# Mask rows in the score stacks, maxima sent round once a batch, and a five-step attention plan on one Trainium2 core

## The reference

```python
xn = _layernorm(x)
x = x + _L0_attn_ref(xn, ...) + _L0_ffn_ref(xn, ...)
xn = _layernorm(x)
x = x + _L1_attn_ref(xn, ...) + _L1_ffn_ref(xn, ...)
# attention, 16 heads of 8 channels, causal (layer 1: 4 key/value heads, rotary)
scores = jnp.einsum('bhqd,bhkd->bhqk', q, k) / jnp.sqrt(D)
scores = jnp.where(causal, scores, -jnp.inf)
out = jnp.einsum('bhqk,bhkd->bhqd', softmax(scores), v)
# experts: 8 of width 512, the top 2 of each token
# layer 0: at most 40 places per expert and batch, relu, softmax gates
# layer 1: no limit, gelu, the two gates by a softmax over their logits
```

## Time and profile before

| | |
|---|---|
| three runs, us | 520.85, 519.69, 522.8; median 520.85 |
| the profiled execution | 522.24 us, span 520.2 us, mean granted clock 0.96 |
| PE busy | 452.7 us, 87% of the span, 3503 matmuls |
| PE weight loads | 343.1 us, 66% |
| DVE | 322.6 us, 62%, 974 instructions |
| ACT | 248.0 us, 48% |
| POOL | 173.7 us, 33% |
| DMA | 45.89 MB, mean 88 GB/s |

### The profile page before, as it was taken

The page is one execution under the profiler, slowest core; times in us unless marked ns, Lnnn a source line. Parts: engine busy times, 40 slices in busy tenths (PEclk is TensorE's granted clock), DMA queues, the critical chain, the costliest instruction groups (busy, mean ns, idle before and its releaser), DMA issues.

```text
span 520.2 us, 10264 instructions
## 1 busy us (share of the span) xinstructions
PE 452.7 (87%) x3503; PEld 343.1 (66%) x3503; DVE 322.6 (62%) x974; ACT 248.0 (48%) x564; POOL 173.7 (33%) x226
## 2 busy tenths in 40 slices
PE   1668899979999999999988987894999999898985
PEld 1554567758868878677665663663999997554643
DVE  5565741126668868777787795642666665565672
ACT  1731455524655655454464442442565563644452
POOL 6640120003254354444544417771000000737600
PEclk9998999997999999999999997896999999899898
DMA  5553123473223233021162612231221211314220
GB/s 163 134 129 89 63 64 107 122 211 114 68 74 99 69 90 115 15 79 42 42 202 95 192 59 70 87 97 56 62 81 44 81 58 36 102 43 135 52 58 28
DMA packets 51441, 45.89 MB, mean 88 GB/s; under 512 B 4968, under 2 KB 46464, under 8 KB 51392
## 3 DMA queue, kind: packets, MB, share of 16 engines
q1 hardware_dynamic: 47424, 35.54, 23.9%
q0 software_dynamic: 2240, 4.53, 3.2%
q10 hardware_dynamic: 1728, 5.20, 3.0%
HBM read 26.24 MB, written 19.01 MB: 87 GB/s over the span
## 4 chain that ended last, share of the span: by engine, by line
PE 49%; issue 23%; DVE 9%; POOL 8%; DMA 5%; ACT 3%; SPq 1%; ACTq 0%; DVEq 0%; POOLq 0%
PE ps_S L1498 7%; PE ps_P L1520 6%; POOL xs L742 6%; PE ps_N L1469 6%; PE ps_N L1465 4%; PE ps_M L1717 3%; PE ps_M L1563 2%; PE ps_M L1600 2%; PE ps_P L1537 2%; DMA X<-in_L_attn_x 2%; PE ps_P L1554 2%; DVE NM L1059 2%; PE ps_N L1710 2%; PE ps_S L1710 2%; PE ps_M L1574 1%
## 5 line engine op out<-in xcount | busy, mean ns | idle before, releaser
L824 ACT ACTIVATE PT<-ps_S 128x512 f32<-128x512 f32 x192 | 112.6, 592 | 98.5 <-PE ps_S L1498 96.6
L1059 DVE TENSOR_REDUCE NM<-ps_N 128x2 f32<-128x512 f32 (+1 forms) x192 | 128.0, 682 | 46.0 <-PE ps_N L1469 44.8
L1469 PE MATMUL ps_N<-STK 96*128 96x256 f32 (+1 forms) x256 | 103.2, 446 | 0.0
L689 POOL TENSOR_SCALAR_AFFINE_SELECT PT<-PT 128x512 f32<-128x512 f32 x80 | 49.1, 638 | 142.5 <-ACT PT L824 142.5
L1498 PE MATMUL ps_S<-STK 100*128 100x128 f32 (+5 forms) x352 | 92.8, 339 | 3.2 <-ACT PT L824 3.2
L1465 PE MATMUL ps_N<-maskb,identb 128*128 128x256 bf16 (+1 forms) x192 | 62.2, 324 | 6.7 <-DVE NM L1059 6.3
L1498 PEld LDWEIGHTS ps_S<-STK 104*128 104x128 f32 (+1 forms) x352 | 62.3, 199 | 7.5 <-ACT PT L824 4.5
L1520 PE MATMUL ps_P<-PT,VA 128*32 128x256 f32 (+1 forms) x1024 | 56.8, 341 | 0.4 <-ACT PT L824 0.4
L1469 PEld LDWEIGHTS ps_N<-STK 96*128 96x128 f32 x256 | 52.0, 203 | 4.7 <-issue 0.7
L731 POOL TENSOR_TENSOR ROT<-ROT 128x256 f32<-128x256 f32 (+1 forms) x16 | 11.3, 731 | 104.2 <-DVE ROT L1088 104.2
L1520 PEld LDWEIGHTS ps_P<-PT,VA 128*32 128x32 f32 x1024 | 27.2, 111 | 26.8 <-issue 12.6
(11 more groups left out here) (197 smaller groups left out, 818.3 us busy)
## 6 DMA issues: line engine op xcount, KB each, us to landing
STK<-scr SPq DMA_DIRECT2D x96, 96.0 KB
scr<-XQ SPq DMA_DIRECT2D x24, 256.0 KB
ROT<-in_L_ffn_W SPq DMA_DIRECT2D x16, 256.0 KB, 3.1
EW<-in_moe ACTq DMA_DIRECT2D x8, 512.0 KB, 3.4
scr<-XQ SPq DMA_DIRECT2D x24, 128.0 KB
xs<-zero SPq DMA_DIRECT2D x1, 2496.0 KB, 11.1
LATE<-xs SPq DMA_DIRECT2D x9, 256.0 KB, 2.8
ysl<-LATE SPq DMA_DIRECT2D x9, 256.0 KB, 2.3
```

Of the source, the lines that this page charges most:

```text
L689: last = pool.affine_select(out=v, in_=v, compare_op=ALU.is_ge, fill=0.0, base=0, pattern=[[0, 4], [1, P]], channel_multiplier=-1)
L824: act.activation(PT[:, g, r, :], bank[s][:], ACT.Exp, scale=SCALE).then_inc(exp_ok, 1)
L1059: dve.tensor_reduce(NM[b % 2][:, h, qt, :].rearrange("q (p c) -> q c p", p=2)[:, slots[0]:slots[-1] + 1, :], bank[s][:].rearrange("q (c p ...
L1469: last = mm(s[:, 2 * w_ * i:2 * w_ * (i + 1)], stk[0:QK_ROWS, c, P * qt:P * (qt + 1)], stk[0:QK_ROWS, k_slots(L, c, 2 * h, 2), 0:w_], star ...
```

## The change

**Mask rows.** The stack's rows 96 to 127 now also carry constants (`constant_rows`, from 512 more columns of the table): rows 104 and up are built so that the product of a query's and a key's row is hugely negative where the key comes after the query. `nat` no longer lays a mask; the diagonal block of 128 keys is multiplied over all 128 rows of the stack, the block left of it over 96. Rows 96 to 103 of the query side have to be zero until the maxima come, so from the fourth batch on SP first copies zeros into them (`L578`).

**Maxima once.** `mxt`, the split, `scm` and the way into the stack handle 16 heads at once, when all twelve units are done: one DMA out and one in, where there were two and four. All of `st` now waits for them.

**The plan.** `st` of a batch runs from unit 4 of its step to unit 3 of the next; `otr`, `ott`, `proj`, `res` come a step later (`e`), `otr` in two halves; there are four buffers of values and two of OT. In steps after the first `qk` stands at unit 2 (was 0), `stack` at unit 5 or 6 (was 1), `mxt` at 0, `px` at unit 4 (was 9), `py` at 6 (4), `po` at 10 (5), `pl` at 7 (10). The slots move from unit 5 to unit 11 of step 12, the scatters to two units each, `moe` from behind step 13 to unit 8 of step 15, and the gathers to one unit each behind it. The plan has 20 steps, was 19.

```diff
+            for i in range(P):
+                for j in range(-(-P // MBLK)):
+                    row, at = ST_ROWS + j, i % MBLK
+                    if i // MBLK == j:
+                        t[row, [CO_KM + i, CO_KM + P + i]] = 2.0 ** (22 * at - 107)
...
-FFN_AFTER, MOE_AFTER = 2, 13
+YC_AT = (9, 11, 15, 17, 22, 25, 40, 44)
+FFN_AFTER, MOE_AFTER = 2, 15
...
         for u in range(12):
-            if u == 0:
+            if u == (0 if first else 2):
                 add("qk", a)
+            if a and u == (0 if first else 3 + 2 * a[0]):
                 add("hi", a)
-            if a and u == a[0]:
+            if a and u == (0 if first else 4 + 2 * a[0]):
                 add("lo", a)
...
             add("nat", b, u)
-            add("st", c, u // 3, u % 3)
+            s, v = (c, u - ST_AT) if u >= ST_AT else (d, u + 12 - ST_AT)
+            add("st", s, v // 3, v % 3)
             add("max", b, u)
...
             if u == 0:
-                add("pv", d, 3)
+                add("mxt", c)
+                add("pv", d, 1)
             if u == 1:
-                add("mxt", c, 1)
-                add("mrow", c, 1)
-                add("stack", a)
-                add("ocp", d, 1)
+                add("mrow", c)
+                add("ocp", d, 0)
+            if u == (1 if first else 5 + a[0] if a else None):
+                add("stack", a)
...
             if u == 4:
-                layer1("py", e)
                 ffn0("disp", g)
                 ffn0("gm", g)
+                layer1("px", k)
...
+            at = 12 * (t - NB - 5) + u
+            if 0 <= at < 2 * NT and at % 2 == 0:
+                plan.append(("scat", at // 2))
+            at = 12 * (t - MOE_AFTER) + u - 9
+            if 0 <= at < NT:
+                plan.append(("back", at))
...
                 if n >= NSTK:
                     await_full(sp, "S1", ("st", *back(L, b, NSTK), 3, 2))
+                    sp.dma_start(stk[QK_ROWS:ST_ROWS, 0:KS, :], stk[0:ST_ROWS - QK_ROWS, KS + 1:KS + 2, :]
+                                 .broadcast_to((ST_ROWS - QK_ROWS, KS, T))).then_inc(stk_in[s], 16)
...
-                diag = s[:].rearrange("q (h k) -> q h k", h=many)[:, :, w_ - P:w_]
-                mm(diag, identb[:], maskb[:, None, :].broadcast_to((P, many, P)), start=True, stop=False,
-                   skip_group_check=True)
                 stk = STK[seq(L, b) % NSTK]
+                q, k = slice(P * qt, P * (qt + 1)), slice(w_ - P, w_)
                 for i, c in enumerate(slots):
-                    last = mm(s[:, 2 * w_ * i:2 * w_ * (i + 1)], stk[0:QK_ROWS, c, P * qt:P * (qt + 1)],
-                              stk[0:QK_ROWS, k_slots(L, c, 2 * h, 2), 0:w_], start=False, stop=True, skip_group_check=True)
+                    o = s[:, 2 * w_ * i:2 * w_ * (i + 1)].rearrange("q (h k) -> q h k", h=2)
+                    if qt > 0:
+                        mm(o[:, :, 0:P], stk[0:QK_ROWS, c, q], stk[0:QK_ROWS, k_slots(L, c, 2 * h, 2), 0:P], start=True, stop=True)
+                    last = mm(o[:, :, k], stk[:, c, q], stk[:, k_slots(L, c, 2 * h, 2), k], start=True, stop=True)
                 last.then_inc(full[f"N{u % 2}"], 1)
```

More of the change, by code:

```diff
@@ L182, in attention_plan @@
                     plan += [("lg",), ("route",)]
[L183 to L191, removed]
-                plan += [("scat", i) for i in range((6, 9, 11, 14, 16)[u // 3], (6, 9, 11, 14, 16)[u // 3 + 1])]
@@ L193, in attention_plan @@
-            if NB + 6 <= t < NB + 9 and u % 3 == 2:
-                k = 4 * (t - NB - 6) + u // 3
-                plan += [("back", i) for i in range(NT * k // 12, NT * (k + 1) // 12)]
-            if t == NB + 8 and u in (6, 8):
-                plan.append(("yc", u // 2 - 3))
-            if t == NB + 9 and u in (0, 2, 4, 6, 7, 9):
-                plan.append(("yc", {0: 2, 2: 3, 4: 4, 6: 5, 7: 6, 9: 7}[u]))
             if u == 4:
-                layer1("py", e)
                 ffn0("disp", g)
@@ L223, in attention_plan @@
             if u == 10:
-                add("ocp", c, 0)
-                layer1("pl", e)
-            if u == 11:
-                add("pv", c, 2)
+                add("otr", d, 1)
+                add("norm", d, 1)
+                layer1("po", h)
+            if t == NB + 4 and u in (8, 9):
+                plan.append(("r1" + "cd"[u - 8],))
+            if t == NB + 4 and u == 10:
+                plan.append(("rank",))
+            if t == NB + 4 and u == 11:
+                plan.append(("slots",))
+            at = 12 * (t - NB - 5) + u
[4 more added lines that the diff above has]
+                plan.append(("back", at))
+            if at in YC_AT:
+                plan.append(("yc", YC_AT.index(at)))
         if t == FFN_AFTER:
             plan.append(("ffn",))
-        if t == MOE_AFTER:
-            plan.append(("moe",))
     return plan
@@ L410, in build @@
         xs, ysl = dram("xs", (NROW, C)), dram("ysl", (NROW, C))
-        scm = [[[dram(f"scm{L}_{b}_{h}", (NH // 2, 2, T)) for h in range(2)] for b in range(NB)] for L in range(2)]
+        scm = [[dram(f"scm{L}_{b}", (2, NH, T)) for b in range(NB)] for L in range(2)]
         full = {n: sem(f"full_{n}") for n in names}
@@ L1291, in evict @@
                     dve.tensor_copy(E_Y[g % 2][:, j % GRP, :], bank[DOWN_BANKS[j % 2]][:, 0:C]).then_inc(ey_ok, 1)
+                dve.wait_ge(x1_ok, sum(1 for x in plan[:plan.index(("moe",))] if x[0] == "res"))
                 for g in range(4):
@@ L1489, in st @@
                 kt = 0 if r < 2 else 1
-                rows = slice(0, QK_ROWS + 4 * (g // 2 + 1))
                 m = 1 if L == 0 else len(slots)
@@ L1497, in st @@
                 for i, c in list(enumerate(slots))[::m]:
-                    last = mm(s[:, n * i:n * (i + m)], stk[rows, k_slots(L, c, g, 1), P * kt:P * (kt + 1)],
-                              stk[rows, c:c + m, T - n:T], start=not masked, stop=True, skip_group_check=masked)
+                    last = mm(s[:, n * i:n * (i + m)], stk[0:ST_ROWS, k_slots(L, c, g, 1), P * kt:P * (kt + 1)],
+                              stk[0:ST_ROWS, c:c + m, T - n:T], start=not masked, stop=True, skip_group_check=masked)
                 last.then_inc(full[f"S{u % 2}"], 1)
@@ L1543, in ott @@
                 await_free(pe, "P0", ("ott", L, b))
-                pe.wait_ge(on_ok, 2 * n + 2)
+                for q in range(TPB):
+                    pe.wait_ge(on_ok[q], n + 1)
                 for q in range(TPB):
```

207 lines of the change are left out of this document (105 added, 102 removed).

## The result

Before 521.74 us (519.69 to 522.80, four runs), after **565.46 us** (563.66 to 567.48, four runs): ratio 1.086, interval [1.080, 1.093]. The forecast was 528 with a range to 543. The direction was right, the size 37 us short. The profiled execution has a span of 563.9 us. Some runs of a kernel are slower than its others; medians here are over all runs and ratios over the fast ones alone, so that a ratio can differ from the quotient of two medians by up to 1%.

The account below looks back on a forecast made before the run. It took PE to bound the attention steps. Savings, new waits and other terms summed to -0.1 on a 520.2 us span, and half clock added 8.4, giving 528.5 of span; it said 528 us, range 503 to 543.

Parts of the forecast that it names:

- TensorE sets the step's length: Attention steps: PE, busy 56.4 of 58.6 us in steps 5 to 7, sets 19.5 and 21.6 us a step.
- the 1.9 us a step saved: PE's gain each step: 1.7 us from maxima units without mask, 0.22 from one pair of transposes less.
- The three waits: New PE waits: projection at unit 2, 1.2 us; XN at unit 4, 2.6; maxima's transposes at unit 0, 1.0.
- 22.3 us a step: Steps 8 to 10: taken in place of the reckoned 23.0, part of the short idle being hidden; +2.3 together.
- rival five: Stack comes 2 us later than reckoned, holding back the first maxima of nine steps: +1.5 each, 541 us, chance 0.05.
- just inside the step: Stack's DRAM road: stack stands at 19 us in layer 0 and 21.7 in layer 1, in time for the step's end.
- the rival I had rightly put first: Rival one, waits and clock: PE's new waits form and bring half clock, 521 to 541 us, chance 0.50.
- my 8.4 for all: Clock term: half clock once in each of steps 5 to 10 behind XN's wait, 1.4 us x 6.
- Rival two: The waits form but the clock holds: 520 us, from 515 to 525, chance 0.20.
- The tail: Behind the expert phase: last store, gathers, additions, last projection and store to out, 51.5 us.
- Rival three: DVE ahead of the reckoned chain, wait at unit 4 under 0.8 us, no half clock: 500 us, chance 0.20.
- Rival four: New maxima units pay by their number of pairs: 0.5 us saved a step and not 1.7, 540 us, chance 0.05.

Follow-up runs that it names:

- e4: Kernel before, own plan, with the mask matmul left out and the maxima's matmuls as pairs of 256 columns: 521.74 us, ratio 1.001.
- e10: Changed kernel with the maxima's units as before (bfloat16 mask matmul, 96 rows): 572.17 us, ratio 1.097.
- e14: Changed kernel with XN ahead of the dispatch mask on DVE in unit 4 and the maxima on bank P1: ratio 1.037.
- e11: Changed kernel with XN ahead of the dispatch mask, maxima on P1, layer 1's early stack and filler matmuls at the stack's waits: 524.20 us, ratio 1.007.
- e1: Changed kernel plus cheap bfloat16 filler matmuls in PE's waits for XN and the stack, no wait removed: 549.86 us, ratio 1.047.
- e12: Changed kernel with XN first, maxima on P1, early stack, fillers at the stack's waits and four more ahead of each XN transposition: 520.48 us, ratio 1.001.
- e6: Changed kernel with XN ahead of the dispatch mask on DVE in unit 4, nothing else: ratio 1.073.
- e2: Changed kernel with PE and ACT turning XN at unit 7 instead of 4, logits at 8, DVE and POOL order kept: 558.15 us, ratio 1.065.
- e5: Changed kernel with XN on DVE and POOL at unit 6, turned on PE at 8, logits at 9: ratio 1.091.
- e15: Changed kernel with XN ahead of the dispatch mask, maxima on P1 and layer 1's early stack, no fillers: ratio 1.038.
- e17: Changed kernel with XN first, maxima on P1, early stack and fillers at the stack's waits and ahead of XN, run again: 519.49 us, ratio 0.997.
- e8: Changed kernel with XN at units 6, 8 and 9, maxima on P1, layer 1's early stack and fillers at the stack's waits: ratio 1.050.
- e13: Changed kernel with XN ahead of the dispatch mask on DVE in unit 4, run on another chip: ratio 1.069.
- e16: Changed kernel with XN first, P1, early stack, all fillers, and the expert phase one step earlier (unit 8 of step 14): ratio 1.023.

## Why the prediction was wrong

**"TensorE sets the step's length" was the step that failed first.** I read 56.4 of 58.6 us busy as the bound and let the 1.9 us a step saved count in full. The PE saving per unit was right (0.11 and 0.22 us). The time was not: e4 gives nothing in the old order, 0.4 us a step in steps 5 to 7, and e10 puts the mask back for 2.6 us in sixteen steps. DVE answers in order, each answer is asked for at a fixed unit, and in e4 a shorter PE mostly waited longer for it. In steps 5 to 7 this error and others cancelled, so that 70.1 met 70.0 by luck; what they were one by one was not taken apart. By size, the two terms that made the 37 us are the stack and the clock, below.

**The three waits:** places right, 0.87, 2.9 and 0.87 us against 0.9, 2.3 and 1.0. The term too small is XN's: 1.3 us for a piece beside POOL's product and not 0.34. Undoing the first and most of the second (e14) brings steps 5 to 7 to 58.5 us between projections, the 58.6 of before. So with the clock behind them they were the whole loss in these steps. In steps 8 to 10 I had also put 22.3 us a step where my own sum gave 23.0, because of idle "hidden in the rows' ends". No run shows that term, and it is 2.1 of the miss of 7.6.

**The stack** was rival five, with 2 us and 0.05. In layer 1 its road began 2 us later and took 1.1 more than reckoned, and at the heads of steps 4, 5 and 11 to 15 PE waited 1.7 to 4.5 us, 20.3 in all. A margin of 0.2 to 3 us, and none in steps 3 and 4, is no cover after a sum of many terms; I had written "just inside the step" and charged nothing. The misses of +3.2, +9.2 and +9.6 lie in the stretches with these waits, and 2.2 us of the +7.6 is one of them.

**The clock** was the rival I had rightly put first, and mis-sized. I charged 3.5 us at half clock in each of six steps, 21 us; the records have 60 more than before. The dips were 3.4, 6.8 and 10.2 us long, and came behind the stack's waits too, in steps for which I had charged none. Not every wait brought one: of the thirteen for XN in steps 5 to 10 and for the stack, two (1.9 us at the head of step 5, 2.96 in step 6) have no half clock behind them, nor have two of e11's of 2.3. e1 gives the price: 15.6 to 21 us in the places where it had fillers, against my 8.4 for all. Rival two, that the clock holds, fell; the Trainium skill's waits of 3 to 5 us ("TensorE: Matmul & The Clock Gate", "HAM oscillation") are longer than the 1.7 and 2.9 us behind which it fell here.

**The tail** took 55.4 and not 51.5. PE waits 1.3 and 4.65 us for the maxima (L1505, DMA STK<-scm). Before the second of these their low part stands on DVE behind an addition of the experts that waits 3.3 us for a gather. In no run was that undone alone.

**Rival three** (DVE ahead of my chain, 0.20) fell. Rival four (pairs count, not columns) fell too: the eight units whose number of matmuls stays at two are 0.11 us shorter all the same, as their columns say.

How the 45 to 49 us of e11 and e12 divide, by the landmark and from a changed kernel at 331 to 339: XN first 12 to 20, P1 6, early stack 11, fillers none to 6; what is left lies behind the landmark. With a scatter of 3 to 8 us between two runs of one kernel, only the first and the sum are clear. What the clock has in each can't be told apart, as each wait removed also removes its dips. Why layer 1's steps lost more clock than layer 0's for the same 2.9 us stays open.

## What to carry to other kernels

A busy share of 96% does not make an engine the bound: where another engine answers in order at fixed places, price a saving by what it lets PE reach, and test it by leaving the work out (e4) before building an order around it. When answers are moved, look at what stands beside them on POOL as well as ahead of them on DVE, and order DVE's queue by who is waiting: one line moved up (e6) did what two relocations (e2, e5) could not. A PE wait of the size of these, 1.7 to 4.5 us, is to be charged twice, once as itself and once as clock behind it: eleven of thirteen here had half clock behind them. A transfer that lands within a couple of us of its use is to be charged as a wait.

## What the runs showed of the hardware

**DVE held up whole by POOL.** A tensor_scalar of 128 x 128 between SBUF tensors takes 0.34 us, 1.30 when a POOL product of 128 x 640 (1.26 us) starts just ahead of it, and 0.62 to 0.67 beside a POOL mask operation of 0.63 us (e5; 0.63 in e11, e12, e15 and e17). The trace shows the hold-up as a longer DVE instruction and not as a wait. The DVE operations ahead of it, with two inputs, ended before the product began, so they say nothing.

**Matmuls that keep the clock up.** Bfloat16 matmuls whose result nobody reads, 0.22 us from start to start, put into the waits kept the granted clock at 2.4 GHz from 140 to 348 us in e1, where the changed kernel has seven dips.

**Chips differ where POOL scatters.** On the chips of e5 to e8 and e13 to e16, 564 and 566 us for a kernel that took 521 on the others, POOL issues its indirect stores in the same 0.96 + 0.30 us, but other engines stand still while they are issued. e8, POOL and then ACT:

```profile
379.00 0.96 POOL L759 DMA_INDIRECT xs<-XN,slot  x1 [0.30 <-issue]
380.26 0.96 POOL L759 DMA_INDIRECT xs<-XN,slot  x1 [0.30 <-issue]
```

```profile
371.62 0.38 ACT L868 ACTIVATE ONT<-ps_P 128x256 f32<-128x256 f32 x1
381.16 0.60 ACT L845 ACTIVATE PT<-ps_S 128x512 f32<-128x512 f32 x1 [9.16 <-issue]
```

ACT waits 9.2 us for nothing that the profile shows, while eight stores are issued; PE waits for ACT. Up to the scatters the two kinds of chip agree: e12 and e16, alike up to step 12, reach its projection at 297.1 and 296.5. The cause was not looked for.
